# Folding the first layer's butterfly stages into its feed-forward matrices, during the attention

## The chip, the cores and the metric

The kernel runs on 1 core of one Trainium2 chip. The metric is the device time of one execution in microseconds (us). The engines of a core work side by side and are tied together by semaphores: TensorE (PE; its weight loads are PEld), VectorE (DVE), ScalarE (ACT), GpSimd (POOL) and SyncE (SP), which issues the DMA transfers. Each engine takes its own instructions in order.

## The reference, cut to what matters

Four layers work on x, 16 sequences of 256 tokens with 128 features. Each layer is `x = x + attention(norm(x)) * silu(feedforward(norm(x)))`. The change concerns the first layer alone:

```python
xn = _layernorm(x)
s = attention(xn)                 # 16 heads of 8, with relative key and query bands of 64
g = silu(ffn(xn))
x = x + s * g

def ffn(x):                       # D_HIDDEN = 512, 9 stages
    h = x @ W_exp + b_exp                       # 128 -> 512
    h = butterfly(h, up_weights, 512)           # up_weights (9, 256, 2, 2)
    h = gelu(h + up_bias)
    h = butterfly(h, down_weights, 512)
    return h @ W_con + b_con + down_bias        # 512 -> 128

def butterfly(y, weights, dim):
    for stage in range(9):                      # linear in y
        s = 2 ** stage; nb = dim // (2 * s)
        a, b = y.reshape(nb, 2, s)[0], [1]      # elements s apart
        w = weights[stage].reshape(nb, s, 2, 2)
        y = stack(w00 * a + w01 * b, w10 * a + w11 * b)
```

Both butterflies are linear. They can be multiplied into W_exp, b_exp and W_con once; the tokens then need only two matrix products and the gelu.

## The kernel before, in words

Everything is float32 with features on the 128 partitions. `build` calls the stages of all layers one after the other; each ends with a barrier of all engines. In the first layer these are `gate_and_norm`, `l0_attention`, `l0_ffn` and `gate_and_norm` again.

`l0_attention` goes through 16 sequences with 4 periods each, 64 periods and 4 to run out. Period p = 4b + r takes four heads of sequence b in four groups g. The order on each engine is written out by hand. For each period:

- TensorE: head products into the logits' banks (`logit`, L451), then per group the key's band (`add_key_band`, L458 to L461, transposes of B) and the transposes of the previous period's probabilities (`transpose`, L482), then the product with v (`weigh`, L495), and at last a new band (`bands`, L440), which waits for VectorE's last `probs_T` copy. Beside them stand the projections qk (r = 2), v and the turned sums (r = 1), the inverted sums' spread (r = 3) and the output projection (r = 0).
- VectorE: per group `add_band` (L633, adds the query's band A and finds the maximum), and for groups 0, 2 and 3 a copy of the previous period's turned probabilities (`turn`, L641). After the groups it copies half of the new band (`keep_band`, L624). At r = 1 a reciprocal of the sums (`invert`, L618) and a copy (L608) come first, at r = 3 the product `o_norm` (L614).
- ScalarE: the exponentials (L565), the copy of group 1's turned probabilities (L573), the other half of the band (L549).
- SyncE: `write(n)` sends band n to memory (L668), `windows(b, j)` fetches it back in slanted windows, four transfers into B and four into A (L687, L696). Band n is made in period n - 6.
- GpSimd: `mask_bands` cuts the windows (L716), `mask_heads(b + 2)` prepares the heads of a later sequence (L732, L734) once all logits of sequence b exist, and stands before the next sequence's masks. The first group of a period waits for its mask.

`l0_ffn` begins when the attention is over. It loads W_exp, b_exp, W_con and the biases, turns W_con by four transposes (L777), and folds the stages: SyncE spreads the weights of one stage for each of the two butterflies over all 128 rows (L803, double buffers); VectorE multiplies and adds, 12 instructions of 128x256 per stage (`stage`, L818 to L820), each waiting for the one before; GpSimd does the same for the one row of the bias, 6 per stage. Two copies, four transposes and four bias columns follow (L832, L852, L854, L860). Then a loop of four passes, each with a block of its own and a barrier, takes two chunks of 512 tokens: 4 products up (L882), 4 gelus (L902), 4 products down (L888), the last sum (L909).

Of the kernel before, what the change touches and what calls it, by code (L numbers as in the profile page):

```python
# [10 lines left out]
ALU = mybir.AluOpType  # L11
# [227 lines left out]
def l0_attention(nc, c, d, x, x_home, xn, s_out, scratch):  # L239
# [8 lines left out]
    with Scope(nc, "a0") as s:  # L248
# [9 lines left out]
        with Scope(nc, "a0t") as t:  # L258
# [100 lines left out]
         y_kept, q_masked, zeroed, masked, key_cut, logits, probs, pt_dve, pt_act, o_kept, inv_ok, *ins_) = s.sems(  # L359
            "qk_mm v_mm st_mm bc_mm y_mm band_mm logit_mm tr_mm pv_mm qk_kept v_kept lo_kept hi_kept st_sb o_ready "  # L360
            "y_kept q_masked zeroed masked key_cut logits probs pt_dve pt_act o_kept inv_ok key_in0 key_in1 key_in2 key_in3 "
            "query_in0 query_in1 query_in2 query_in3 row_out0 row_out1 row_out2 row_out3")
        key_in, query_in, row_out = ins_[:NG], ins_[NG:2 * NG], ins_[2 * NG:]
        tile = (slice(0, P), slice(P, NK))
# [27 lines left out]
        with nc.Block() as block:  # L392
# [209 lines left out]
            def _(dve):  # L602
# [39 lines left out]

                for n in range(6):
                    keep_band(n)
                for p in range(LAST + 1):
# [4 lines left out]
                    for g in range(4):  # L650
                        if p < NQ:
                            add_band(p, g)
                        if 1 <= p <= NQ and g != 1:
                            turn(p - 1, g)
                    if band_of(p) is not None:
                        keep_band(band_of(p))

            @block.sync
            def _(sp):
# [37 lines left out]

                for n in range(4):
                    write(n)
                for b in range(NSEQ):  # L700
                    for j in range(3):
                        windows(b, j)
                    if b + 1 < NSEQ:
                        write(4 * b + 4)
                        write(4 * b + 5)
                    windows(b, 3)
                    if b + 1 < NSEQ:
                        write(4 * b + 6)
                        write(4 * b + 7)
# [38 lines left out]
def l0_ffn(nc, c, d, xn, g_out):  # L748

    F, ST = 512, 9
    NF = F // P
    with Scope(nc, "f0") as s:
        up = s.sb("up", [P, F])
        dn = s.sb("dn", [P, F])
        upb = s.sb("up_bias", [1, F])
        one = s.sb("one", [1, 1])  # L760
        wc = s.sb("W_con", [P, NF, P])
        down = s.sb("down", [P, NF, P])
        bias_up = s.sb("bias_up", [P, NF])
        bias_out = s.sb("bias_out", [P, 2])
        bo = s.sb("bo", [P, 1])
        load(nc, s, [(up[:], d["W_exp"]), (upb[:], d["b_exp"].rearrange("(a n) -> a n", a=1)),
                     (wc[:], d["W_con"].rearrange("(c p) n -> p c n", p=P)), (bias_up[:], column(d["up_bias"])),
                     (bias_out[:, 0:1], column(d["b_con"])), (bias_out[:, 1:2], column(d["down_bias"]))])

        with Scope(nc, "f0t") as t:  # L770
            ps = t.banks("ps")
            turned, kept = t.sems("turned kept")
            with nc.Block() as block:
                @block.tensor
                def _(pe):
                    for i in range(NF):
                        nc.tensor.transpose(ps[:, 0, i * P:(i + 1) * P], wc[:, i, :], c["ident"][:]).then_inc(turned, 1)  # L777

                @block.vector
                def _(dve):  # L780
                    nc.vector.memset(one[:], 1.0)
                    nc.vector.tensor_tensor(bo[:], bias_out[:, 0:1], bias_out[:, 1:2], ALU.add)
                    dve.wait_ge(turned, NF)
                    nc.vector.tensor_copy(dn[:], ps[:, 0, :]).then_inc(kept, 1)
            t.barrier()

        with Scope(nc, "f0b") as t:
            wt = t.sb("stage_w", [P, 2, 2, 2 * F])
            tmp = t.sb("tmp", [P, 2, F])
            alt = t.sb("alt", [P, 2, F])  # L790
            btmp = t.sb("btmp", [1, F])
# [2550 lines left out]
```

## Time and profile before

| | us |
|---|---|
| median of 3 runs | 4407.21 (4401.78 to 4411.33) |
| the profiled execution's own time | 4403.99 |
| its span | 4402.1 |
| attention of the first layer, last result | 556.45 |
| first instruction of the next norm | 733.90 |

Busy shares of the span: PE 81%, PEld 58%, DVE 60%, ACT 48%, POOL 39%; the granted clock of TensorE is 0.907 of full speed on average. Times in the rows count from the start of the span. The span is that of the profiled execution; its own time is 1.9 us more. A timeline row has start, duration, engine, line, operation, output<-inputs, and in brackets how long the engine stood idle before and whose result ended it. A windows row has the stretch, its length, then busy time and instructions of PE, PEld, DVE, ACT and POOL, the granted clock (1.00 is 2.4 GHz, 0.50 is 1.2 GHz), the DMA engines' mean busy share and GB/s.

### The profile page before, as it was taken

The page shows a single profiled execution, that of the slowest core. Times are in us where ns is not written, and L with a number is a line of the kernel's source. Part 1 is how long each engine was busy: PE and PEld are TensorE (multiplying, and loading weights), DVE is VectorE, ACT ScalarE, POOL GpSimd, SP SyncE. Part 2 cuts the span into 40 slices and gives each one's busy share as a digit, 9 for nine tenths or more (in the row PEclk, how much of TensorE's full clock was granted, in tenths as well). Part 3 has the DMA queues.
Part 4 walks back from the last instruction along what each step waited for, and adds up shares of the span by engine and source line. Part 5 has one row for each costly group of instructions (what it writes and reads, how often), then busy time and mean ns, then how long its engine had stood idle before and what let it go on. Part 6 is the DMA issues. An engine that isn't in the chain of part 4 may idle for free. (4 is left out here: it accounts for less than half of the span.)

```text
span 4402.1 us, 79023 instructions
## 1 busy us (share of the span) xinstructions
PE 3562.2 (81%) x26972; PEld 2564.8 (58%) x26972; DVE 2629.4 (60%) x6366; ACT 2108.2 (48%) x5657; POOL 1698.5 (39%) x1896
## 2 busy tenths in 40 slices
PE   5888807656999978999996888884999999995581
PEld 2555603433666645666664888772777777774461
DVE  3666672433666645666664666663788888885233
ACT  4666604333665643544444444444666666661120
POOL 3554540303666643333330000000666666672505
PEclk7999958877999998999998999997999999996795
DMA  3777620012000000000001000001222222223122
GB/s 110 205 197 184 174 91 0 9 33 45 1 1 1 2 6 6 2 1 2 1 2 39 0 0 0 0 0 35 66 76 76 76 76 73 76 78 107 57 69 63
DMA packets 232672, 224.58 MB, mean 51 GB/s; under 512 B 59209, under 2 KB 176905, under 8 KB 232074
## 3 DMA queue, kind: packets, MB, share of 16 engines
q1 hardware_dynamic: 225642, 206.52, 16.9%
q0 software_dynamic: 4096, 8.40, 0.6%
q10 hardware_dynamic: 2592, 5.26, 0.3%
q8 instruction: 195, 3.19, 0.3%
q14 instruction: 147, 1.20, 0.1%
HBM read 166.10 MB, written 54.00 MB: 50 GB/s over the span
## 5 line engine op out<-in xcount | busy, mean ns | idle before, releaser
L2159 DVE TENSOR_TENSOR_SCAN a_h<-a_dA,a_dBu_psum 128x512 f32<-128x512 f32 x512 | 595.9, 1205 | 164.5 <-issue 105.0
L1160 POOL TENSOR_SCALAR a_probs<-a_probs,a_row_inv 128x128 f32<-128x128 f32 (+1 forms) x512 | 381.3, 762 | 324.0 <-DVE a_row_inv L1146 324.0
L2116 POOL TENSOR_TENSOR a_h<-a_h,main_g 128x512 f32<-128x512 f32 x256 | 385.1, 1506 | 270.4 <-DVE a_h L2159 260.3
L1658 DVE SCALAR_TENSOR_TENSOR m_acc<-m_o_psum,m_gate,m_acc 128x128 f32<-128x128 f32 x992 | 297.8, 346 | 116.9 <-PE m_o_psum L1622 116.5
L1883 PE MATMUL a_dBu_psum<-a_B_diag,a_dt_u_turned 64*128 64x128 f32 x4096 | 317.0, 289 | 21.6 <-DVE a_h L2159 20.8
L1622 PEld LDWEIGHTS m_o_psum<-m_values,m_hidden 128*128 128x128 f32 x2048 | 313.9, 197 | 30.0 <-ACT m_hidden L1640 2.6
L1614 PE MATMUL m_h_psum<-m_x,m_keys 128*128 128x256 f32 x1024 | 327.8, 411 | 0.0
L1640 ACT ACTIVATE m_hidden<-m_h_psum 128x256 f32<-128x256 f32 x512 | 196.2, 383 | 265.0 <-PE m_h_psum L1614 265.0
L1622 PE MATMUL m_o_psum<-m_values,m_hidden 128*128 128x128 f32 x2048 | 314.5, 280 | 0.0
L1485 POOL TENSOR_TENSOR r_position_q<-r_turned_q 128x512 f32<-128x512 f32 x128 | 159.9, 1271 | 388.9 <-DVE r_turned_q L1530 388.9
L1442 ACT ACTIVATE r_probs<-r_logits_psum,r_neg_max 128x256 f32<-128x256 f32 x512 | 235.1, 475 | 140.4 <-DVE r_neg_max L1536 140.4
L1883 PEld LDWEIGHTS a_dBu_psum<-a_B_diag,a_dt_u_turned 64*128 64x128 f32 x4096 | 257.8, 188 | 76.0 <-issue 71.2
L1904 PE MATMUL a_y_psum<-main_ident,a_h 128*128 128x128 f32 x2048 | 275.3, 276 | 7.7 <-POOL a_h L2116 6.7
L1536 DVE TENSOR_REDUCE r_neg_max<-r_logits_psum 128x2 f32<-128x512 f32 x256 | 165.0, 686 | 180.8 <-PE r_logits_psum L1352 180.8
L1904 PEld LDWEIGHTS a_y_psum<-main_ident,a_h 128*128 128x128 f32 x2048 | 230.2, 141 | 68.3 <-issue 45.8
L565 ACT ACTIVATE a_probs<-a_logits,a_neg_max 128x128 f32<-128x128 f32 (+1 forms) x512 | 225.6, 443 | 89.7 <-DVE a_neg_max L633 89.7
L1352 PE MATMUL r_logits_psum<-r_key_trig,r_position_q 64*128 64x256 f32 x2048 | 255.5, 389 | 0.0
L1753 POOL MEMSET a_flip<- 128x128 f32 x1 | 0.2, 204 | 656.1 <-POOLq L52 656.1
L1104 ACT ACTIVATE a_probs<-a_logits,a_neg_max 128x128 f32<-128x128 f32 (+1 forms) x512 | 225.2, 444 | 3.0 <-DVE a_neg_max L1126 2.2
L2023 ACT ACTIVATE a_dA<-a_dt,a_b_A 128x510 f32<-128x510 f32 x256 | 165.7, 712 | 102.1 <-DVE a_h L2159 101.4
L2023 ACT ACTIVATE a_dA<-a_dt,a_f_A 128x510 f32<-128x510 f32 x256 | 165.6, 711 | 95.2 <-DVE a_h L2159 94.4
L1352 PEld LDWEIGHTS r_logits_psum<-r_key_trig,r_position_q 64*128 64x128 f32 x2048 | 187.4, 186 | 38.6 <-issue 21.5
(540 smaller groups left out, 8244.4 us busy)
## 6 DMA issues: line engine op xcount, KB each, us to landing
main_g<-a_b_c_rows SPq DMA_DIRECT2D x256, 256.0 KB, 3.1
a_band_rows<-main_g SPq DMA_DIRECT2D x64, 512.0 KB, 3.4
a_B<-a_band_rows SPq DMA_DIRECT2D x192, 128.0 KB, 3.2
a_A<-a_band_rows SPq DMA_DIRECT2D x192, 128.0 KB, 3.1
f_x_rows<-f_zero ACTq DMA_DIRECT2D x16, 320.0 KB, 9.3
f_x_expert<-f_x_rows SPq DMA_DIRECT2D x16, 320.0 KB, 2.8
f_y_rows<-f_y_expert SPq DMA_DIRECT2D x16, 320.0 KB, 2.2
f0b_stage_w<-L_ffn_up_weights SPq DMA_DIRECT2D x9, 512.0 KB, 4.3
```

The source lines that it names most:

```text
L565: nc.scalar.activation(pr[:, k % 2, g, tile[t]], lg[:, k % 2, g, tile[t]], ACT.Exp, scale=-1.0, bias=nmax[:, k % 2, g, t:t + 1], accum_out ...
L1160: ins = nc.gpsimd.tensor_scalar(pr[:, h % NPR, tile[t]], pr[:, h % NPR, tile[t]], rinv[:, p % NST, q:q + 1], None, ALU.mult)
L1352: ins = mm(lb[:, 2 * i + a, t * T:(t + 1) * T], g_[r, k % NGB, i, half, t * P:(t + 1) * P], key_trig[r, half, :], start=False, stop=t == 1 ...
L1442: nc.scalar.activation(pr[:, k % 2, g, t, :], lb[:, g, t * T:(t + 1) * T], ACT.Exp, bias=nmax[:, k % 2, g, t:t + 1], accum_out=sums[:, b % ...
L1614: nc.tensor.matmul(hp[:, e % 3, 0:T], keys[:, e, :], tile_x[:], start=True, stop=True).then_inc(h_mm, 1)
L1622: ins = nc.tensor.matmul(op[:, f % 3, t * P:(t + 1) * P], hs[:, f % NH, t * P:(t + 1) * P], vals[:, f, :], start=True, stop=True)
L1658: ins = nc.vector.scalar_tensor_tensor(out=acc[:, t, :], in0=o, scalar=gate[:, t, e:e + 1], in1=acc[:, t, :], op0=ALU.mult, op1=ALU.add)
L1883: ins = mm(dst[:, :, tc * P + HALF * half:tc * P + HALF * (half + 1)], dtuT[U % 2][rows, q, tc, k * P:(k + 1) * P], diag[rows, M % NDIAG, ...
L1904: ins = mm(yT[:, q, tc * DI + k * P:tc * DI + (k + 1) * P], h[:, (NK * g + k) % NH, n, tc * P:(tc + 1) * P], c["ident"][:], start=False, s ...
L2023: ins = ac(dA[:, M % NDA, :, k, n, 1:], by_seq(dt[U % 2][:, k, :])[:, :, 1:], ACT.Exp, scale=W[U % 2]["A"][:, k, 2 * m + n:2 * m + n + 1])
L2116: tt(h[:, r, :, :], h[:, r, :, :], Cs[:, g % NCS, :, :], ALU.mult).then_inc(hc_pool, 1)
L2159: nc.vector.tensor_tensor_scan(flat, dA[:, M % NDA, q, k, :, :].rearrange("p n t -> p (n t)"), db[:, 2 * (g % 2) + k, :], 0.0, ALU.mult, A ...
```

## The change

A class `Butterfly` holds the tables, in buffers that exist beside the attention's. Its `ops` are 162 instructions: for each of the 9 stages 12 that alternate between `up` and the one row of `up_bias` (six each), then six for `down`. Per six the kinds are multiply, multiply, add, twice. `weights(h)` is the transfer of half-stage h (18 of them), of 512 KB, into one of two buffers. In the attention VectorE takes one op after group 0, one after group 2 and one after the band copy, in periods 0 to 53. Each op waits for the one before by a counter; the first also waits for the six loads, and the first of a half-stage for its weights. SyncE issues loads and the first two weights after `windows(0, 0..2)`, and the other 16 behind a band's write, after a wait for the counter. The bias row's work moves from GpSimd to VectorE. W_con is handed over transposed, so the first transposes go. `l0_ffn` keeps only the turning of `down`, the bias columns and the products; its eight chunks stand in one block, without loop.

```diff
+class Butterfly:
+        self.ops = []
+        for h in range(2 * self.ST):
+            i, k = h // 2, h % 2
+            for n in range(6):
+                for what in ("down",) if k else ("up", "up_bias"):
+                    self.ops.append((h, what, self.ST - 1 - i if k else i, i, n))
+    def first_of(self, h):
+        return sum(1 for op in self.ops if op[0] < h)
+    def loads(self):
+        d = self.d
+        return [(self.up[:, 0, :], d["W_exp"]), (self.down[:, 0, :], d["W_conT"]),
+                (self.up_bias[:, 0, :], d["b_exp"].rearrange("(a n) -> a n", a=1)), (self.bias_up[:], column(d["up_bias"])),
+                (self.bias_out[:, 0:1], column(d["b_con"])), (self.bias_out[:, 1:2], column(d["down_bias"]))]
+    def weights(self, h):
+        i, k = h // 2, h % 2
+        src = self.d["down_weights"][self.ST - 1 - i] if k else self.d["up_weights"][i]
+        return self.w[:, h % 2, :], src.rearrange("k r c -> (k r c)").unsqueeze(0).broadcast_to([P, 2 * self.F])
+    def turn(self, eng, op):
...
+        if n % 3 == 0:
+            return eng.tensor_tensor(m[:, :, r, :], weight(1), y[:, :, 1, :], ALU.mult)
+        if n % 3 == 1:
+            return eng.tensor_tensor(o[:, :, r, :], weight(0), y[:, :, 0, :], ALU.mult)
+        return eng.tensor_tensor(o[:, :, r, :], o[:, :, r, :], m[:, :, r, :], ALU.add)
 # l0_attention, VectorE
+                def turn_table():
+                    n, op = next(ops, (None, None))
+                    if op is None:
+                        return
+                    h = op[0]
+                    if n == 0:
+                        dve.wait_ge(table_in, 16 * len(tables.loads()))
+                    if n == tables.first_of(h):
+                        dve.wait_ge(weight_in[h % 2], 16 * (h // 2 + 1))
+                    if n:
+                        dve.wait_ge(turned_op, n)
+                    tables.turn(nc.vector, op).then_inc(turned_op, 1)
...
                         if 1 <= p <= NQ and g != 1:
                             turn(p - 1, g)
+                        if g % 2 == 0 and p < NQ:
+                            turn_table()
                     if band_of(p) is not None:
                         keep_band(band_of(p))
+                    if p < NQ:
+                        turn_table()
 # l0_attention, SyncE
+                def put_weights(h):
+                    if h >= 2:
+                        sp.wait_ge(turned_op, tables.first_of(h - 1))
+                    dst, src = tables.weights(h)
+                    sp.dma_start(dst, src).then_inc(weight_in[h % 2], 16)
+                def write_and_load(n):
+                    write(n)
+                    while due[0] is not None and (tables.first_of(due[0] - 1) - 1) // 3 <= n - 6:
+                        put_weights(due[0])
+                        due[0] = next(halves, None)
                 for b in range(NSEQ):
                     for j in range(3):
                         windows(b, j)
+                    if b == 0:
+                        for dst, src in tables.loads():
+                            sp.dma_start(dst, src, allow_slow_non_contiguous=True).then_inc(table_in, 16)
+                        put_weights(0)
+                        put_weights(1)
                     if b + 1 < NSEQ:
-                        write(4 * b + 4)
-                        write(4 * b + 5)
+                        write_and_load(4 * b + 4)
+                        write_and_load(4 * b + 5)
                     windows(b, 3)
...
 # l0_ffn, what is left
+                pe.wait_ge(made, 1)
+                for f in range(NF):
+                    nc.tensor.matmul(tp[:, 1, f:f + 1], upb[:, f * P:(f + 1) * P], one[:], start=True,
+                                     stop=True).then_inc(biased, 1)
+                for f in range(NF):
+                    nc.tensor.transpose(tp[:, 0, f * P:(f + 1) * P], dn[:, f * P:(f + 1) * P], c["ident"][:]).then_inc(turned, 1)
+                raise_(0)
+                pe.wait_ge(kept, 2)
+                for k in range(NCH):
+                    if k + 1 < NCH:
+                        raise_(k + 1)
+                    lower(k)
```

## Rows read from the trace of the kernel before

**Rows 1.** Window of the attention: us, busy us (instructions) by engine, clock, DMA share, GB/s.

```profile
83.00:556.00 473.00, 408.74 (x4008) 280.56 (x4005) 294.51 (x1320) 316.75 (x1221) 241.95 (x448) 0.97 0.72 189
```

**Rows 2.** Timeline of VectorE, 271 to 364 us: start, duration, [idle before, releaser].

```profile
271.65 0.69 DVE L624 COPY main_g<-a_transposed_psum 128x512 f32<-128x512 f32 x1 [1.31 <-PE a_transposed_psum L440]
...
278.93 0.69 DVE L624 COPY main_g<-a_transposed_psum 128x512 f32<-128x512 f32 x1 [1.31 <-PE a_transposed_psum L440]
...
285.71 0.69 DVE L624 COPY main_g<-a_transposed_psum 128x512 f32<-128x512 f32 x1 [1.31 <-PE a_transposed_psum L440]
289.44 0.29 DVE L633 CUSTOM_DVE_ANT_0 a_logits<-a_logits_psum,a_A 128x128 f32<-128x128 f32 x1 [3.04 <-POOL a_A L716]
...
294.46 0.69 DVE L624 COPY main_g<-a_transposed_psum 128x512 f32<-128x512 f32 x1 [1.31 <-PE a_transposed_psum L440]
295.07 0.34 DVE L618 RECIPROCAL a_sums<-a_sums 128x32 f32<-128x32 f32 x1
...
301.33 0.69 DVE L624 COPY main_g<-a_transposed_psum 128x512 f32<-128x512 f32 x1 [1.31 <-PE a_transposed_psum L440]
...
355.71 0.69 DVE L624 COPY main_g<-a_transposed_psum 128x512 f32<-128x512 f32 x1 [2.26 <-PE a_transposed_psum L440]
...
363.71 0.69 DVE L624 COPY main_g<-a_transposed_psum 128x512 f32<-128x512 f32 x1 [1.31 <-PE a_transposed_psum L440]
```

**Rows 3.** Timeline of TensorE, 284 to 291 us and 353 us.

```profile
284.55 1.13 PE L440 MATMUL a_transposed_psum<-a_rq_blocks,a_k 64*128 64x512 f32 x4 [0.64 <-DVE a_probs_T L641]
...
290.70 0.52 PE L482 MATMUL a_transposed_psum<-main_ident,a_probs 128*128 128x128 f32 x3 [1.80 <-DVE a_probs_T L641]
...
353.60 2.08 PE L440 MATMUL a_transposed_psum<-a_rk_blocks,a_q 64*128 64x512 f32 x4 [0.28 <-DVE a_probs_T L641]
```

**Rows 4.** Timeline of GpSimd, 282 to 289 us.

```profile
282.98 0.92 POOL L732 TENSOR_SCALAR a_k_shifted<-a_k,a_shift_k 128x256 f32<-128x256 f32 x1 [10.31 <-PE a_logits_psum L461]
...
286.95 2.37 POOL L716 TENSOR_SCALAR_AFFINE_SELECT a_A<-a_A 128x256 f32<-128x256 f32 x4
```

**Rows 5.** Timeline of the stage boundary, 555 to 558 us.

```profile
555.98 0.47 ACT L543 ACTIVATE main_s<-a_project_psum,a_vectors 128x256 f32<-128x256 f32 x1 [1.49 <-PE a_project_psum L421]
557.32 0.34 SPq L106 DMA_DIRECT2D f_up<-L_ffn_W_exp  x1
```

**Rows 6.** Timeline of VectorE in the butterfly stages, 584 to 587 us.

```profile
584.31 1.05 DVE L818 TENSOR_TENSOR f0b_tmp<-f0b_stage_w,f0b_alt 128x256 f32<-128x256 f32 x1
585.39 0.61 DVE L819 TENSOR_TENSOR f_up<-f0b_stage_w,f0b_alt 128x256 f32<-128x256 f32 x1
586.03 0.43 DVE L820 TENSOR_TENSOR f_up<-f_up,f0b_tmp 128x256 f32<-128x256 f32 x1
```

**Rows 7.** Timeline from the folded matrices to the next norm.

```profile
663.69 0.69 DVE L860 COPY f_down<-f0c_ps_psum 128x512 f32<-128x512 f32 x1 [4.72 <-PE f0c_ps_psum L854]
...
683.97 7.13 PE L882 MATMUL f_hidden_ps_psum<-main_xn,f_up 128*128 x16 [2.29 <-PEq L52]
...
698.13 0.75 DVE L909 TENSOR_SCALAR main_g<-f_y_psum,f_bo 128x512 f32 x1 [2.68 <-PE f_y_psum L888]
...
733.90 1.28 ACT L141 ACT_TABLE_LOAD   x1 [7.88 <-PEq L52]
```

**Rows 8.** Timeline of VectorE and of SyncE's DMA issues, start of the attention.

```profile
82.68 0.29 DVE L633 CUSTOM_DVE_ANT_0 a_logits<-a_logits_psum,a_A 128x128 f32<-128x128 f32 x1 [1.73 <-PE a_logits_psum L461]
...
86.06 2.55 SPq L696 DMA_DIRECT2D a_A<-a_band_rows  x4
```

**Rows 9.** Waits of SyncE's queue, 100 to 530 us (total, times, longest).

```profile
SPq L667 <- DVE main_g L624: 62.3, 14, 7.0
```

**Rows 10.** The stage weights' transfers before, from issue to landing.

```profile
DMA to landing us min/median/max: 4.2/5.4/7.4
```

**Rows 11.** Two windows of 20 us.

```profile
340.00:360.00 20.00, 17.29 (x145) 11.45 (x141) 11.43 (x51) 10.70 (x42) 14.24 (x27) 0.83 0.81 218
2460.00:2480.00 20.00, 15.73 (x87) 14.12 (x86) 11.64 (x44) 8.31 (x18) 0.00 (x0) 0.83 0.00 0
```

More of the change, by code:

```diff
@@ L241, in l0_attention @@
+def l0_attention(nc, c, d, tables, xn, s_out, scratch):
     WIN, HD, NG = 64, 8, 4
@@ L641, in turn @@
                     nc.vector.tensor_copy(pt[:, k % 2, g, :], tb[:, g % 2, 0:NK]).then_inc(pt_dve, 1)
+                ops = iter(enumerate(tables.ops))
+                def turn_table():
[10 more added lines that the diff above has]
+                    tables.turn(nc.vector, op).then_inc(turned_op, 1)
                 for n in range(6):
@@ L696, in windows @@
                         sp.dma_start(dst, src).then_inc(query_in[j], 16)
+                def put_weights(h):
[3 more added lines that the diff above has]
+                    sp.dma_start(dst, src).then_inc(weight_in[h % 2], 16)
+                halves = iter(range(2, 2 * tables.ST))
+                due = [next(halves)]
+                def write_and_load(n):
[3 more added lines that the diff above has]
+                        due[0] = next(halves, None)
                 for n in range(4):
@@ L745, in l0_attention, with l0_ffn @@
         s.barrier()
[L748 to L754 removed]
+def l0_ffn(nc, c, tables, xn, g_out):
+    F = tables.F
     NF = F // P
[L756 to L759, printed above, removed]
+    up, dn, upb = tables.up[:, 1, :], tables.down[:, 1, :], tables.up_bias[:, 1, :]
+    with Scope(nc, "f0m") as s:
         one = s.sb("one", [1, 1])
[L761 to L791, printed above, removed]
[L792 to L862 removed]
@@ L864, in l0_ffn @@
+        down = s.sb("down_T", [P, NF, P])
+        bias_up, bo = tables.bias_up, s.sb("bo", [P, 1])
         W = BANK
+        NCH = xn.shape[1] // W
         hid = s.sb("hidden", [P, 2, NF, W])
@@ L914, in l2_attention @@
+        s.barrier()
 def l2_attention(nc, c, d, xn, s_out):
@@ L3310, in build @@
         gate_and_norm(nc, c, x, xn)
-        l0_attention(nc, c, part("L0_attn"), x, d["x"], xn, s, g)
-        l0_ffn(nc, c, part("L0_ffn"), xn, g)
+        with Scope(nc, "f0") as f:
+            tables = Butterfly(f, part("L0_ffn"))
+            l0_attention(nc, c, part("L0_attn"), tables, xn, s, g)
+            l0_ffn(nc, c, tables, xn, g)
         gate_and_norm(nc, c, x, xn, s, g, gate=True)
```

180 lines of the change are left out of this document (71 added, 109 removed).

## The prediction

> **What bounds the kernel now.** I read the stage boundaries in the timeline first: the attention ends at 556.45, the next norm begins at 733.90 [rows 5, 7], and barriers part both from the rest, so the change acts up to 734 us and nothing behind it moves. What can be won is read between these two times. What must be paid is read in the attention, where the added work goes: its window shows all engines half to four fifths busy [rows 1], which tells nothing yet, since what counts is what sets its pace.
>
> VectorE's timeline answers this. Its copy of a band (L624) comes once a period, and its starts are 7.28, 6.78, 8.75 and 6.87 us apart, 29.7 us for a sequence of four periods [rows 2]; it repeats so for all 16. Three of the four periods have one loop: VectorE takes the four head groups in one piece of 3.7 us (289.44 to 294.46 less the 1.31 waited); its last copy of probs_T releases TensorE's bands, which had waited 0.64 us for it [rows 3]; bands, logits and the key's first band lead back to VectorE. So VectorE's piece lies on the path, though it is busy only 62% of the attention [rows 1]. The step of 8.75 is set by GpSimd (call the position of a period in its sequence r; this is the way from r = 3 to r = 0): its heads and masks run from 282.98 to 289.32 [rows 4], and VectorE waits 3.04 us for them [rows 2]. There TensorE waits 1.80 us [rows 3].
>
> **What it removes, after the attention.** From the attention's last result (555.98 + 0.47 = 556.45, rows 5) to the next norm's first instruction (733.90, rows 7) are 177.4 us. Of this the loads, the first transposes, the 18 half-stages, two copies and their barriers go. What stays:
> - start of a block, 0.9 us from 556.45 to 557.32 [rows 5], taken as 1.1;
> - four bias columns and four transposes: VectorE waited 4.72 for them, block start of 0.9 included, so 3.8 [rows 7];
> - eight chunks without barriers between them. A pair takes 683.97 to 698.13 = 14.16 [rows 7], of which 0.44 is the way to VectorE; four times 13.72 is 54.9. The present loop pays barrier and table load on each pair;
> - a slow clock at the start, 2.2, estimated from bands at 2.08 against 1.13 [rows 3] over four us of work; I take it in full, as the end of the attention leaves TensorE waiting;
> - the way to the last copy, the copy and the way to the norm: 0.44 + 0.75 + 0.8 = 2.0.
>
> Sum 64.0, so 113.5 are removed. If the clock stays up at the start, the 2.2 and half of the 3.8 go too, 117.
>
> **What it adds inside the attention: 162 VectorE instructions**, 108 on 128 rows and 54 on one row (same 256 columns, so the same time), three a period over periods 0 to 53. Alone, a multiplication takes 0.61 and an addition 0.43 [rows 6]. Neighbours of other tiles overlap by 0.08 (294.46 + 0.69 against 295.07, rows 2), so they add 0.53 and 0.35. The order of the list gives only multiplications to the first slot (after group 0), four of six to the second (after group 2), two of six to the third (after the band copy). The first two slots are inside the piece on the path: 0.53 + 0.47 = 1.0 a period. The third falls into VectorE's wait for the next key band (a period of 7.28 less 3.7, 1.31 and 0.69 leaves 1.6; one of 6.78 leaves 1.1, 0.4 of it taken by o_norm) or for GpSimd; only where the reciprocal of the sums follows at once (295.07), once in four periods, does it cost 0.42 [rows 2].
>
> Beside GpSimd the same multiplication took 1.05 instead of 0.61 [rows 6]: where both engines work, one waits for the other's instruction. In the attention GpSimd is busy half of the time [rows 1] and in runs, from r = 3 through r = 0 and part of r = 1. A VectorE instruction meets one under way in about five slots of twelve; the wait is the rest of a GpSimd instruction, which takes 0.6 (four in 2.37, rows 4), so some 0.28. Two of these collisions are in the chain of 282.98 to 289.32 and make it longer by 0.5 each. (The Trainium skill, SBUF — State Buffer, Who interferes with whom, says that a VectorE instruction with two SBUF inputs and a GpSimd one that reads SBUF exclude each other for the whole instruction. By this rule the collisions count; were they free, the sum per sequence would be 3.4 instead of 5.3. The trace agrees: 1.05 against 0.61.)
>
> Per sequence: r = 0: 1.0 + 0.55; r = 1: 0.42 + 1.0 + 0.28; r = 2: 1.0; the GpSimd period: 1.0 (VectorE's own way there has 1.8 us to spare, as TensorE's wait of 1.80 shows, which covers its slots). Sum 5.25, over 53 periods = 13.25 sequences: 70 us. Bounds: 45 without any collision (3.42 a sequence); 130 if every instruction costs what it cost beside a busy GpSimd, 1.0 (2.0 in each of three periods, 0.9 before the reciprocal, 2.9 in GpSimd's chain).
>
> **What it moves: the loads.** SyncE issues windows of sequence 0 until 88.6 [rows 8]; the six loads and the first weights stand behind them. VectorE's first added instruction stands behind group 0 of period 0, at about 83.4 (82.68 and two reductions, rows 8), and waits for both. Six loads take some 2.7 us to issue (0.34 the first, rows 5, those of columns more), and weights landed 5.4 us after issue, 4.2 to 7.4 [rows 10]. So the first weights are there at 88.6 + 2.9 + 5.4 = 96.9, and VectorE stands for 13 us with groups 1 to 3 behind it, and ScalarE and TensorE behind those. GpSimd gets ahead meanwhile, so its hold on the early periods (up to the 3.04 of rows 2) goes into it, and the half clock after so long a pause adds something: 12 net, 9 to 17.
>
> The other 16 weight transfers (0.5 MB each, 8.4 MB where the attention moves 189 GB/s times 473 us = 89 MB, rows 1) I cost at nothing. SyncE waits 62.3 / 14 = 4.4 us a sequence for bands now [rows 9]; each transfer is issued about two periods (14 us) before its first use and lands in 4 to 7. SyncE's new wait, for VectorE's counter, is for an instruction one further than the band that it has just written, so about 1 us; windows stand behind it, GpSimd's masks wait for those, but GpSimd's critical chain starts from the logits and not from a window (282.98 waited for logits_psum, rows 4). If that cover went, each of 16 would cost some 5 us.
>
> **The clock.** TensorE's clock fell to half in four of the fourteen periods with the 1.80 us wait; the bands then took 2.08 instead of 1.13 [rows 3], and the next period 8.00 instead of 6.87 (355.71 to 363.71, rows 2): 2.1 us together. After the change TensorE waits 1.6 to 2.0 us in every period. All the attention is at 0.97 now [rows 1]; the stretch of this fall is at 0.83, so 0.17 x 2 x 20 = 6.8 us at half clock cost 2.1, 0.3 each; a later stage where TensorE is busy 79% is at 0.83 too [rows 11]. TensorE's busy share goes from 86% to some 75%: nothing to 36 us more (0.86 of clock over some 550 us instead of 0.97, so 120 us more at half). I take 12, since only four waits of this length in fourteen brought the clock down, and some of the cost falls where GpSimd sets the pace.
>
> **Sum.** -113.5 + 70 + 12 + 12 = -19.5. The profiled execution took 4403.99 (span 4402.1, 1.9 around it), so 4384.5; the median of before is 3.2 above its profiled execution, so 4387.7; I predict 4387.
>
> **Rivals.**
> - *The collisions cost little* (GpSimd's instructions let VectorE's through, or fall elsewhere): -113.5 + 45 + 12 + 8 = -48, 4359. For it: most of GpSimd's work of a sequence lies in one run. Against it: rows 6. Chance 0.16.
> - *The clock falls in most periods*: -113.5 + 70 + 14 + 36 = +6, 4413, no change. For it: the clock of 0.83 where TensorE is busy for a like share [rows 11]. Against it: ten of fourteen waits of 1.80 us left it alone. Chance 0.17.
> - *The other side: VectorE and GpSimd serialise.* If each added instruction meets a GpSimd one, as it did in the table stages, the attention pays 130 and the result is -113.5 + 130 + 12 + 12 = +40, 4447. It decides from 7 us a sequence on, against my 5.25. Against it: GpSimd is idle in half of the slots. With partly met ones (from 4416): chance 0.14.
> - *The change hides everything* (the slots fill VectorE's idle 38%): about 4300. Against it: TensorE's waits for the last copy in each period [rows 3]. Chance 0.03.
>
> **How the numbers follow.** My forecast has 0.50, its own range 4370 to 4404, the others 0.16, 0.17, 0.14 and 0.03. The clock and collision rivals together bring the range for 8 in 10 to 4352 to 4425. This kernel's measurement tells 0.2%, 8.8 us, from no change: 4398.4 to 4416. Faster: 0.43 of my forecast, 0.05 of the clock's, 0.16 and 0.03, together 0.67; same: 0.07 of mine, 0.11 of the clock's, 0.18; slower: 0.01 + 0.14, 0.15.
>
> **What the profile will show.** The stretch from the attention's last result to the next norm at 62 to 66 us, TensorE without a gap of more than 1 us in it. A wait of VectorE of 12 to 14 us near 83 us for the weights' transfer. Steps of the band copy of about 8.6, 8.3, 8.0 and 10.0 instead of 6.9, 7.3, 6.8 and 8.75 while the tables are made, and the old ones in the last ten periods. Added multiplications at 0.61 where GpSimd rests and up to 1.2 where it works. I am wrong if the steps grow by under 0.8 or over 2 a period, if the clock of the attention is below 0.9, or if VectorE waits for weights after the first ones.

## The result, and the profile after

The changed kernel takes 4358.22 us (median of four runs, 4349.31 to 4360.85) against 4404.49 for the kernel before beside it (4396.62 to 4411.33): ratio 0.9892, 95% interval 0.9869 to 0.9915. It is faster by about 46 us, or 1.1%, where I forecast 20, and lies below my own range of 4370 to 4404, inside the one for 8 in 10 (4352 to 4425). Its profiled execution took 4349.31, so the two profiled executions are 54.7 apart; that difference is what is taken apart below.

The attention's window and the stretch behind it, changed kernel (columns as in rows 1):

```profile
83.00:556.00 473.00, 349.54 (x3373) 241.34 (x3372) 332.08 (x1273) 280.75 (x1034) 231.21 (x394) 0.96 0.73 189
624.00:685.00 61.00, 58.26 (x140) 26.45 (x140) 7.03 (x12) 23.12 (x35) 0.00 (x0) 0.97 0.00 0
```

In the same 473 us TensorE and ScalarE did less than in [rows 1] (349.54 us against 408.74), VectorE more: the attention is stretched. The clock is 0.96 against 0.97, and the mean DMA rate is the same 189 GB/s.

VectorE's timeline, first the start, then one sequence of four periods; L684 is the band copy, L291 to L294 are the added instructions:

```profile
82.27 0.42 DVE L693 CUSTOM_DVE_ANT_0 a_logits<-a_logits_psum,a_A 128x256 f32<-128x256 f32 x1
82.61 0.08 DVE L693 DVE_READ_ACCUMULATOR2_ANT a_neg_max<- 128x1 f32 x1
96.53 0.61 DVE L291 TENSOR_TENSOR f_tmp<-f_stage_w,f_up 128x256 f32<-128x256 f32 x1 [13.83 <-DMA f_stage_w<-L_ffn_up_weights]
...
209.48 0.69 DVE L684 COPY main_g<-a_transposed_psum 128x512 f32<-128x512 f32 x1 [1.31 <-PE a_transposed_psum L500]
...
212.77 0.62 DVE L291 TENSOR_TENSOR f_tmp<-f_stage_w,f_up 128x256 f32<-128x256 f32 x1
...
214.88 0.59 DVE L291 TENSOR_TENSOR f_bias_tmp<-f_stage_w,f_up_bias 1x256 f32<-1x256 f32 x1
...
217.80 0.69 DVE L684 COPY main_g<-a_transposed_psum 128x512 f32<-128x512 f32 x1 [1.31 <-PE a_transposed_psum L500]
218.41 0.60 DVE L293 TENSOR_TENSOR f_up<-f_stage_w,f_up 128x256 f32<-128x256 f32 x1
...
225.43 0.69 DVE L684 COPY main_g<-a_transposed_psum 128x512 f32<-128x512 f32 x1 [1.31 <-PE a_transposed_psum L500]
...
228.71 0.29 DVE L693 CUSTOM_DVE_ANT_0 a_logits<-a_logits_psum,a_A 128x128 f32<-128x128 f32 x1 [1.99 <-PE a_logits_psum L521]
...
231.85 0.71 DVE L293 TENSOR_TENSOR f_down<-f_stage_w,f_down 128x256 f32<-128x256 f32 x1
...
234.89 0.69 DVE L684 COPY main_g<-a_transposed_psum 128x512 f32<-128x512 f32 x1 [1.31 <-PE a_transposed_psum L500]
...
243.29 0.69 DVE L684 COPY main_g<-a_transposed_psum 128x512 f32<-128x512 f32 x1 [1.31 <-PE a_transposed_psum L500]
```

The stall at the start is there, 13.83 us, for the weights. Then the band copies are 8.32, 7.63, 9.46 and 8.40 us apart, where [rows 2] has 7.28, 6.78, 8.75 and 6.87. Two of the three added instructions of a period stand ahead of the last copy of probs_T, the third behind the band copy. Behind period 53, without table instructions, the last four steps are the old ones (577.64 to 584.50 is 6.86). Of the signs that I named for being wrong, VectorE waits for no weights after the first ones, the clock is over 0.9, and the steps grow by 1.03 in the mean, though the one behind 225.43 by 0.71, under my 0.8.

TensorE's timeline, same kernel:

```profile
224.26 1.13 PE L500 MATMUL a_transposed_psum<-a_rq_blocks,a_k 64*128 64x512 f32 x4 [1.48 <-DVE a_probs_T L701]
229.97 0.52 PE L542 MATMUL a_transposed_psum<-main_ident,a_probs 128*128 128x128 f32 x3 [1.45 <-DVE a_probs_T L701]
233.73 1.13 PE L500 MATMUL a_transposed_psum<-a_rk_blocks,a_q 64*128 64x512 f32 x4 [1.78 <-DVE a_probs_T L701]
```

Its wait for VectorE's last copy was 0.64 [rows 3] and is now 1.48 in the same place: the two slots ahead of that copy add to the path.

GpSimd's timeline, same kernel, and its groups over 100 to 570 us (the last columns are busy us, mean ns):

```profile
221.84 0.92 POOL L833 TENSOR_SCALAR a_k_shifted<-a_k,a_shift_k 128x256 f32<-128x256 f32 x1 [11.82 <-PE a_logits_psum L521]
222.74 2.39 POOL L835 TENSOR_SCALAR a_q_masked<-a_q,a_mask,a_shift_q_masked 128x256 f32<-128x256 f32 x4
225.09 0.99 POOL L817 TENSOR_SCALAR_AFFINE_SELECT a_B<-a_B 128x512 f32<-128x512 f32 x2
226.05 2.54 POOL L817 TENSOR_SCALAR_AFFINE_SELECT a_A<-a_A 128x256 f32<-128x256 f32 x4
```

```profile
L817 POOL TENSOR_SCALAR_AFFINE_SELECT a_A<-a_A 128x512 f32<-128x512 f32 x159 | 107.2, 690 | 7.6
L835 POOL TENSOR_SCALAR a_q_masked<-a_q,a_mask,a_shift_q_masked 128x256 f32<-128x256 f32 x56 | 33.6, 612 | 0.0
```

The chain from the first head to the end of the fourth mask of A takes 226.05 + 2.54 - 221.84 = 6.75 us, against 6.34 in [rows 4]. Between these two ends the kernel before has:

```profile
283.88 2.16 POOL L734 TENSOR_SCALAR a_q_masked<-a_q,a_mask,a_shift_q_masked 128x256 f32<-128x256 f32 x4
285.99 1.00 POOL L716 TENSOR_SCALAR_AFFINE_SELECT a_B<-a_B 128x512 f32<-128x512 f32 x2
```

So the masked heads are longer by 0.23 us and the masks of A by 0.17 (2.54 against 2.37), the rest is as before. A mask of A takes 690 ns in the mean; with the same filter over 100 to 550 us of the kernel before it was 634, a masked head 555. Of the 162 table instructions 85 run while one of GpSimd's does.

VectorE's own instructions hardly suffer (counts, then min/median/max ns):

```profile
L291 DVE TENSOR_TENSOR f_tmp<-f_stage_w,f_up x18: 606/620/640, 96.5 to 524.1; 128x256 f32<-128x256 f32 x18
L291 DVE TENSOR_TENSOR f_tmp<-f_stage_w,f_down x18: 615/626/1001, 128.4 to 549.6; 128x256 f32<-128x256 f32 x18
```

The end of the attention and the feed-forward, by ScalarE, VectorE and TensorE:

```profile
623.53 0.47 ACT L603 ACTIVATE main_s<-a_project_psum,a_vectors 128x256 f32<-128x256 f32 x1 [1.49 <-PE a_project_psum L481]
...
684.84 1.28 ACT L141 ACT_TABLE_LOAD   x1 [7.65 <-PEq L52]
```

```profile
625.08 1.05 PE L885 MATMUL f0m_turned_psum<-f0m_one,f_up_bias 1*128 1x1 f32 x8 [1.58 <-DVE f0m_one L909]
626.05 1.01 PE L888 MATMUL f0m_turned_psum<-main_ident,f_down 128*128 128x128 f32 x4
626.85 8.41 PE L872 MATMUL f0m_hidden_ps_psum<-main_xn,f_up 128*128 128x512 f32 x16
```

```profile
645.60 0.75 DVE L918 TENSOR_SCALAR main_g<-f0m_y_psum,f0m_bo 128x512 f32<-128x512 f32 x1 [6.04 <-PE f0m_y_psum L880]
652.47 0.75 DVE L918 TENSOR_SCALAR main_g<-f0m_y_psum,f0m_bo 128x512 f32<-128x512 f32 x1 [6.12 <-PE f0m_y_psum L880]
```

The attention ends at 624.00, 67.6 later than before [rows 5]; the next norm begins at 684.84. The stretch between is 60.84, under my 62 to 66, against 177.45 [rows 5, 7]. TensorE's one gap of over 1 us in it is the first, 1.58. A chunk takes 6.87 us.

**The balance** between the two profiled executions, with attention steps summed from the starts of the band copies. "Regular" is 13 sequences at the median of each of the four steps; what the same 52 steps took beyond it is "irregular".

```
                                         forecast   measured
stretch after the attention               -113.5     -116.6
regular steps (per sequence 5.25 / 4.13)   +70        +53.7
start                                      +12        +15.2
irregular steps (forecast: the clock)      +12         +0.1   (6.8 after, 6.7 before)
first copy and tail of the attention         0         -1.3
all behind the next norm                     0         -5.6
sum                                        -19.5      -54.5   (-54.7 unrounded)
```

### The profile page after: what moved, and what is told of

Read it like the earlier page. It is cut to its first block and busy times, and to the rows that moved or that the text cites. A ratio compares the mean times of both kernels' runs of the same rounds, so it can differ in the third digit from the quotient of the medians.

```text
span 4347.6 us, 78783 instructions
## 1 busy us (share of the span) xinstructions
PE 3550.6 (82%) x26968; PEld 2561.0 (59%) x26968; DVE 2628.9 (60%) x6417; ACT 2116.3 (49%) x5654; POOL 1665.8 (38%) x1841
```

## The experiments

The kernels below were timed in three groups, each beside runs of the kernel before, and ratios are to those. Those took 4431.0 us for the first four kernels below, 4404.27 for the next four and 4434.39 for the last two, so times of different groups, and the times in us that I expected, are compared by ratio or stage. "Steps" are the medians to r = 2, 3, 0, 1; in the kernel before they are 7.28, 6.78, 8.75, 6.86, in the changed one 8.33, 7.63, 9.46, 8.39.

**Loads ahead of the pipeline.** The six loads and first two weight transfers are issued before SyncE's loop and not inside it.

```diff
+                for dst, src in tables.loads():
+                    sp.dma_start(dst, src, ...).then_inc(table_in, 16)
+                put_weights(0)
+                put_weights(1)
...
-                    if b == 0:
-                        for dst, src in tables.loads(): ...
-                        put_weights(0)
-                        put_weights(1)
```

> Only the six loads and the first two weight transfers move: SyncE issues them before the first band's write instead of after the first twelve window transfers. My theory (VectorE's wait of 13.8 us near 83 us is for these transfers alone, and 15 us of the attention's 67.5 us are its price): the wait is gone, the attention ends 12 to 15 us earlier, time about 4344. Rival (the windows and GpSimd's masks set the pace of the first periods anyway, VectorE waited 3.4 us for them in period 1 before the change): the gain is 11 us or less. Second rival (the early transfers delay the first bands' way): the first group of period 0 starts later than 82.05.

Measured: 4369.24 us, ratio 0.9857 (0.9842 to 0.9872). The stall is gone: the two steps from 80 us on take 14.8 us together where the changed kernel needs 28.9 and the kernel before 13.8. But the attention ends at 615.47, only 8.5 earlier: under the 12 to 15 of the theory and in the range of the rival, though not by its cause, since the two steps gave 14.1 back. The ratio's interval overlaps that of the changed kernel. Regular steps are unchanged (33.86 us a sequence); irregular ones take 11.3 us beyond them, where the changed kernel had 6.8. Two of them, 9.64 and 10.34, follow each other from 171 us on, where the clock is at 0.66 (170 to 180 us).

**Slots moved into waits.** Of the three table instructions of a period, two are issued between the last copy of probs_T and the band copy, and one behind that.

```diff
-                        if g % 2 == 0 and p < NQ:
-                            turn_table()
+                    if p < NQ:
+                        turn_table()
+                        turn_table()
                     if band_of(p) is not None:
                         keep_band(band_of(p))
```

> The same 162 instructions, other places: two after VectorE's last copy of a period and before the band copy, where it waits 1.31 us for TensorE, one after the band copy as before. My theory (the cost is the two slots inside the piece that TensorE waits for): the steps of the band copy go back to about 6.9 + 0.4, 7.3, 6.8 and 8.75 to 9.1, the attention is some 45 us shorter, time about 4313, and the wait at the start costs a few us less, since it stands behind period 0's groups. Rival (VectorE's work itself or its meeting with GpSimd costs, wherever it stands): the steps stay at 9.5, 8.4, 8.3 and 7.7, time about 4358.

Measured: 4332.49, ratio 0.9780 (0.9765 to 0.9795); steps 7.28, 6.78, 9.43, 7.38, the attention ends at 573.98. The same 162 instructions cost nothing at two of the four steps. What is left is 0.7 us at the GpSimd step, over the 0 to 0.35 that I expected and what the rival had there, and 0.5 at the step with the reciprocal. Of the 50.0 us by which the attention ends earlier, 38.4 are these steps, 5.0 the start (the wait for weights is 11.23 instead of 13.83) and 6.2 irregular steps, of which 0.3 us are left.

**Both together.**

> Both edits of the two runs before. If their costs are independent: the attention ends 10 to 15 us before that of the slots alone, time 4295 to 4303. If GpSimd or the windows become the limit, the steps of the first sequence stay long and the time is above 4308.

Measured: 4324.90, ratio 0.9761 (0.9748 to 0.9775), attention's end 565.20, 8.8 before that of the moved slots alone where I expected 10 to 15; steps 7.28, 6.78, 9.42, 7.38. VectorE's timeline of it, around a band copy:

```profile
301.22 0.61 DVE L291 TENSOR_TENSOR f_tmp<-f_stage_w,f_down 128x256 f32<-128x256 f32 x1
301.87 0.61 DVE L293 TENSOR_TENSOR f_down<-f_stage_w,f_down 128x256 f32<-128x256 f32 x1
302.62 0.69 DVE L684 COPY main_g<-a_transposed_psum 128x512 f32<-128x512 f32 x1
303.22 0.42 DVE L294 TENSOR_TENSOR f_down<-f_down,f_tmp 128x256 f32<-128x256 f32 x1
303.56 0.35 DVE L678 RECIPROCAL a_sums<-a_sums 128x32 f32<-128x32 f32 x1
```

Where 1.31 us were waited for TensorE's band [rows 2] stand two multiplications. On VectorE only the addition ahead of the reciprocal (303.22) delays something. The GpSimd step is longer by what GpSimd's chain is longer: 0.67 and 0.66 (7.00 us against 6.34). The two groups that are slower in it:

```profile
229.59 2.65 POOL L835 TENSOR_SCALAR a_q_masked<-a_q,a_mask,a_shift_q_masked 128x256 f32<-128x256 f32 x4
232.20 1.17 POOL L817 TENSOR_SCALAR_AFFINE_SELECT a_B<-a_B 128x512 f32<-128x512 f32 x2
```

**Two weight transfers only.** The other 16 are not issued; the table instructions go on with the weights of the first two transfers.

```diff
-                    if n == tables.first_of(h):
+                    if n == tables.first_of(h) and h < 2:
...
-                halves = iter(range(2, 2 * tables.ST))
+                halves = iter(range(0))
```

> The changed kernel without the 16 later weight transfers: all half-stages multiply with the first two weights (left out: the other weights, so the tables are others). My theory (these transfers are hidden): every step of the band copy as in the changed kernel within 0.1 us, time 4350 to 4362. Rival (the transfers slow the windows, GpSimd's masks wait longer, and SyncE's wait for VectorE's counter holds back windows): the attention ends 5 us or more earlier.

Measured, one run: 4377.50, attention's end 621.58 against 624.00, steps 8.33, 7.64, 9.47, 8.43. The steps are those of the changed kernel; 2.4 us is within what its irregular steps vary by.

**No table instructions, all transfers.** SyncE waits for the transfer before in the same buffer instead of for VectorE's counter.

```diff
-                            turn_table()
...
-    up, dn, upb = tables.up[:, 1, :], tables.down[:, 1, :], tables.up_bias[:, 1, :]
+    up, dn, upb = tables.up[:, 0, :], tables.down[:, 0, :], tables.up_bias[:, 0, :]
```

> The changed kernel with all transfers of the tables and weights kept, but none of VectorE's 162 table instructions; the first layer's feed-forward takes the unmultiplied matrices, so its result leaves the butterfly out. Theory (the attention's added time outside the start is those instructions, the transfers are hidden): the band copies' steady steps return to 7.28, 6.78, 8.75 and 6.87 us, the attention ends at 558 to 566 us (before: 556.5; with the instructions and two weight transfers: 621.6). Rival (the transfers cost time of their own beside the attention): steps stay over those by 0.2 us or more each, and the end lies at 575 or later. The next layer norm follows 60 to 61 us after the attention's end in both.

Measured, one run: 4287.85; steps 7.28, 6.79, 8.75, 6.86; attention's end 554.58, just below the 558 to 566 expected, the next norm at 615.4. The 16 later weight transfers beside the attention cost nothing that shows. The loads at the start do: one step, from 100.02 to 111.75, is 11.73 us long where the kernel before has 6.37. GpSimd and VectorE in it:

```profile
102.45 1.00 POOL L816 TENSOR_SCALAR_AFFINE_SELECT a_B<-a_B 128x512 f32<-128x512 f32 x2 [9.20 <-DMA a_B<-a_band_rows]
106.73 0.29 DVE L693 CUSTOM_DVE_ANT_0 a_logits<-a_logits_psum,a_A 128x128 f32<-128x128 f32 x1 [6.02 <-PE a_logits_psum L521]
```

SyncE issues the six loads and two weights from 87.99 to 92.15 us, the windows stand behind them, and GpSimd waits for the windows: these masks begin at 102.45, against 95.75 in the kernel before and 95.84 with the loads ahead of the pipeline. In the changed kernel VectorE's stall of 13.83 us covers this.

**The product's one block alone**, in the kernel before.

```diff
-        PER = 2
-        with nc.Fori(0, xn.shape[1] // (W * PER) or 1) as i:
-            per = min(PER, xn.shape[1] // W)
-            with nc.Block() as block:
+        NCH = xn.shape[1] // W
+        with nc.Block() as block:
...
-                    for k in range(per):
+                for k in range(NCH):
```

> The kernel before with one part of the change alone: the feed-forward's two products with their eight chunks in one block, in place of a block of their own each time; the butterfly stages stay passes over the activations after the attention. Theory (my sum gave some 10 us of the stretch after the attention to this part): the stretch from the attention's end to the next table load falls from 177.4 to 166 to 168 us, and the ratio to the kernel before is 0.9974 to 0.9980. Rival (all of the 116.6 us comes from the nine passes up and nine down that go away): 176 to 178 us, ratio 0.9995 to 1.0005.

Measured: the stretch is 717.9 - 549.9 = 168.0 as the theory had it, 9.4 less. But the whole takes 4405.08, ratio 1.0001 (0.9992 to 1.0010), and in its profile the later stages take the gain back in small pieces (first to third table load 2243.8 us instead of 2235.6). The stretch is the theory's, the ratio the rival's (0.9995 to 1.0005); neither foresaw both.

**Table instructions with one input.**

```diff
-            return eng.tensor_tensor(m[:, :, r, :], weight(1), y[:, :, 1, :], ALU.mult)
+            return eng.tensor_scalar(m[:, :, r, :], weight(1), 0.5, None, ALU.mult)
(and so the other two)
```

> The changed kernel with each of the 162 table instructions turned into a product of the same strided stage weight with a constant, written to the same place: one input from SBUF in place of two, same count, places in the order, waits and shape of result; the matrices are left out of the table, so the result is not the butterfly's. Theory (the part of the step to r = 0 that is over 8.75 us, +0.71, is GpSimd made slower while VectorE reads two inputs from SBUF, its chain 6.75 against 6.34 us): GpSimd's short masks are back at 1.00 us, the chain at 6.3 to 6.45, the step to r = 0 at 8.75 to 8.9, and the other three stay over their old values by the instructions' own durations (if these stay at 0.6 us: 8.3, 7.6, 8.3; if one input takes half the time: about 7.9, 7.2, 7.6). Rival (GpSimd is late for another reason, its later start behind VectorE or the DMA traffic): the chain stays at 6.7 to 6.8 and the step to r = 0 at 9.3 to 9.5.

Measured: 4345.25, ratio 0.9862 (0.9847 to 0.9877); steps 7.87, 7.38, 9.52, 8.05. Undisturbed the instruction takes 0.39 instead of 0.62, and three steps shrink by 0.46, 0.25 and 0.34. The GpSimd step does not. GpSimd's timeline of it:

```profile
221.07 1.25 POOL L833 TENSOR_SCALAR a_k_shifted<-a_k,a_shift_k 128x256 f32<-128x256 f32 x1 [10.00 <-PE a_logits_psum L521]
222.31 2.17 POOL L835 TENSOR_SCALAR a_q_masked<-a_q,a_mask,a_shift_q_masked 128x256 f32<-128x256 f32 x4
224.43 1.00 POOL L817 TENSOR_SCALAR_AFFINE_SELECT a_B<-a_B 128x512 f32<-128x512 f32 x2
225.38 2.53 POOL L817 TENSOR_SCALAR_AFFINE_SELECT a_A<-a_A 128x256 f32<-128x256 f32 x4
```

The chain is 6.84 long here, and so in nine of thirteen sequences; in four it is 6.54. The rival's numbers came out within 0.04, though not for its reason: the slowed instruction is now the first (1.25 instead of 0.92), a one-input instruction holds GpSimd up as well, and without any table instruction the step is 8.75. Over the whole attention it holds it up less: a mask of A takes 660 ns in the mean, against 690 with two inputs and 634 before.

**The third slot away from the reciprocal**, on top of the version with both: none behind the band copy of r = 0, two behind that of r = 3.

```diff
                     if p < NQ:
-                        turn_table()
+                        for _ in range((0, 1, 1, 2)[p % NG]):
+                            turn_table()
```

> The version with the loads ahead and two table instructions ahead of each band copy, and of the third ones, the one that stands ahead of the reciprocal of the sums is moved to behind the r = 3 copies, where VectorE waits 3.3 us for a mask. Theory (the step to r = 1 is still long by 0.5 us because the reciprocal and all behind it start one instruction late): that step goes from 7.38 to 6.9, the others stay at 7.26, 6.78 and 9.5, the attention ends at 558 to 560 us in place of 565.2, the ratio to the kernel before is 0.9745 to 0.975. Rival (the moved instruction hits GpSimd's masks there and lengthens its chain by what the other step gains): the step to r = 0 at 9.8 to 10.0, the attention's end within 2 us of 565.

Measured: 4296.22, ratio 0.9752 (0.9739 to 0.9766); steps 7.28, 6.78, 9.73, 6.86; attention's end 563.65. Its GpSimd timeline:

```profile
226.81 0.92 POOL L834 TENSOR_SCALAR a_k_shifted<-a_k,a_shift_k 128x256 f32<-128x256 f32 x1 [6.17 <-PE a_logits_psum L521]
227.72 2.73 POOL L836 TENSOR_SCALAR a_q_masked<-a_q,a_mask,a_shift_q_masked 128x256 f32<-128x256 f32 x4
230.40 1.36 POOL L818 TENSOR_SCALAR_AFFINE_SELECT a_B<-a_B 128x512 f32<-128x512 f32 x2
231.72 2.36 POOL L818 TENSOR_SCALAR_AFFINE_SELECT a_A<-a_A 128x256 f32<-128x256 f32 x4
```

The step to r = 1 is at its old length, as the theory said, but the instruction set down in VectorE's wait meets the masked heads (2.73 where the version with both has 2.65) and the short masks (1.36 for 1.17). The chain is 7.27 long instead of 7.00 and the GpSimd step 0.3 longer: most of the gain goes back, and the attention ends 1.6 earlier, within the rival's 2. The interval overlaps that of the version with both; each of the two beats both kernels.

**The products in four blocks again**, in the changed kernel, and **the changed kernel unedited** beside it. The diff is that of the one block alone, reversed, with the bias columns and transposes in a block ahead.

> The changed kernel with the feed-forward's products in the form of the kernel before (four blocks of two chunks each, the bias and transposes in a block ahead of them); the attention and the tables as changed. The kernel before with one block of eight chunks had its stretch shortened by 9.3 us, but its whole time was the same (ratio 1.0001, interval 0.9992 to 1.0010). Theory (the one block is worth some 9 us of the stretch, and something behind it gives them back): the stretch from the attention's end to the next table load is 70 to 72 us in place of 60.8, and the ratio to the kernel before lies within 0.001 of that of the changed kernel on the same chip. Rival (the 9 us reach the end here, and the missing gain of the other run was a chance of its later stages): the same stretch, and a ratio 0.002 over that of the changed kernel.

> The changed kernel without any edit, on the same chip as the version with four blocks, as what that is compared with: ratio 0.987 to 0.991, attention's end at 618 to 626 us, stretch 60.8 us, the time from the table load behind it to the next two 2230 to 2245 and from there to the end 1426 to 1438 us (so far these two varied in that way between kernels whose later stages are the same).

Measured: 4391.80, ratio 0.9907 (0.9892 to 0.9921), stretch 693.45 - 620.18 = 73.3; unedited 4382.97, ratio 0.9884 (0.9868 to 0.9901), stretch 691.06 - 630.23 = 60.8. The medians are 8.8 us apart, as the rival has it, but the intervals overlap. In the unedited kernel the attention ended at 630.23, outside what I expected, with 11.6 us of irregular steps, and the stages from the third table load on took 1454.6 us against the 1426 to 1438 expected. The kernel before is slower in this group too. In all profiles of this group and the first these last stages take 1452 to 1459 us, in the others, the two of the first comparison and the second group, 1429 to 1437. Where the irregular steps lie, the windows of the unedited kernel show (the last columns are the clock, DMA share, GB/s):

```profile
284.00:340.00 56.00, 41.34 (x413) 28.50 (x413) 40.01 (x154) 33.04 (x121) 30.36 (x52) 1.00 0.83 206
340.00:400.00 60.00, 48.87 (x396) 35.13 (x395) 40.73 (x154) 34.40 (x129) 20.42 (x35) 0.83 0.63 162
400.00:440.00 40.00, 30.35 (x304) 20.43 (x303) 27.93 (x104) 23.34 (x85) 22.63 (x39) 1.00 0.68 171
```

From 337 to 385 us, most of it in the window with a clock of 0.83, five steps took 9.19, 9.78, 9.58, 10.47 and 8.98 instead of 8.4, 8.32, 7.64, 9.49 and 8.4. TensorE is busy 48.87 of 60 us there; that it is the bound in such a stretch fits, but no run took it apart. In all these profiles, every step over 0.5 us longer than usual either has a granted clock below 1.00 or follows right behind one that has; the step of 11.73 us above has its own cause.

## Why the forecast was right in sign and short in size

**What bounds the attention** was read rightly. VectorE's piece sets three steps: its instructions cost their length inside the piece and nothing in its waits (slots moved: 7.28 and 6.78 again; no instructions: all four old steps). GpSimd sets the fourth.

**The stretch** was -113.5 and is -116.6. The chunks and the way out were priced right: from the first up-product 58.0 us (626.85 to 684.84) against 54.9 + 2.2 + 2.0 = 59.1. The bias and the transposes with the block's start took 2.85 (624.00 to 626.85) against 4.9; I had taken the old wait of 4.72 [rows 7], in which transposes and products alternated with the clock at half.

**The step that failed is the price of collisions in the per-sequence sum**, 5.25 against 4.13: of the 35 us between forecast and measured balance, 16 lie here and 12 in the clock. The steps to r = 2, 3, 0, 1 grew by 1.05, 0.85, 0.71 and 1.52; I had named steps of 8.3, 8.0, 10.0 and 8.6, which grow by 5.15 and do not match my sum one by one. The sum has 1.0 for r = 2 and 1.7 for the step with the reciprocal, both near what came; its other 2.55, for r = 0 and the GpSimd chain, stand against the 1.56 of the steps to r = 3 and 0. I lengthened the chain by 1.0 (two collisions of 0.5). Both collisions came, at 0.23 and 0.17, and it grew by 0.41 (6.75 against 6.34). The rest of that step's growth is VectorE's piece: behind the masks it takes 6.18 us (228.71 to 234.89) instead of 5.02 (289.44 to 294.46, rows 2), while the chain starts 3.59 instead of 2.73 ahead of the band copy. I had also let VectorE wait 0.28 in five of twelve slots; 85 of 162 instructions do meet one of GpSimd's, so the share was right, but VectorE's multiplications kept a median of 0.62. The price is paid mostly by GpSimd (690 ns a mask against 634), which has time to spare except in its chain. The table stages of the kernel before were the wrong row to price this from: there two engines, both without any pause, did the same two-input work. The Trainium skill (SBUF — State Buffer, Who interferes with whom) says that the losing engine is locked out for the whole instruction; here what a meeting with a two-input instruction adds to a group of GpSimd's is 0.17 and 0.23 us in the chain of the changed kernel, less than the 0.6 of the instruction met. A meeting can begin late in either instruction, so this does not refute the rule; it shows that my half microsecond was too much, and no run came near my 130 us bound.

**The start**, 12, was 15.2 (the wait itself 13.83, forecast 13). I had netted some of it against GpSimd's lead; the runs do not show such a gain. That it is the loads' place in the queue is shown by the first experiment, which took the wait away. That this bought 8.5 us and not 14 is mostly from irregular steps (4.5 us more of them), whose sum varied from run to run. What the forecast left out is that the loads also push back the windows behind them, which cost 5.4 us in the run without table instructions and is hidden under the wait here.

**The clock**, 12, was nothing in this execution: irregular steps 6.8 us against 6.7 before. The waits of TensorE that I forecast came, 1.0 to 2.0 us in every period, but they did not lower its clock much more often (0.96 against 0.97). A long fall does cost: the five steps of the unedited kernel's second profile are 5.8 us over their usual length. Over the profiles with the slots of the changed kernel (unedited twice, early loads, two transfers, four blocks) irregular steps are 3.1, 4.0, 6.8, 11.3 and 11.6 us. At the old pace they are 6.7 in the kernel before, 1.5 in its version with one block, and 1.9 without table instructions, the step of 11.73 left out. The means are 7.4 and 3.4, so the term is nearer 4 than 12, and single executions put it at -4 to +10; that it came to nothing in the two executions compared is chance. In the two versions with moved slots, where TensorE waits 0.64 us again in most periods, irregular steps are 0.3 and 0.0. What tips the clock is not settled: in the changed kernel a wait of 1.96 us at 438.92 stood ahead of a window at 0.89 (440 to 460 us), one of 1.78 at 233.73 ahead of one at 1.00 (240 to 260 us).

**Nothing behind the norm moves**: the profiled executions differ by 5.6 us there, 1.4 of it from first to third table load and 4.0 behind. In all the kernels here, which share that code, the first part took 2232.7 to 2243.8 us, and the second 1428.6 to 1437.2 in those timed beside a kernel before of 4404; the difference is within this scatter. The medians are 46.3 apart and the profiled executions 54.7: that of the changed kernel, 4349.31, was the fastest of its four.

**What stays open** is the worth of the product's one block. Its stretch is 9 to 12 us shorter in both pairs; in the kernel before nothing of this reached the end, in the changed kernel 8.8 us did, with overlapping intervals. A cause was not found, and scatter of the later stages explains the profile of the first pair but not the median of its ten runs. What tips the clock, and so the irregular steps, is open too.

Of the rivals, "the collisions cost little" came nearest (4359), though by a middle sum of collisions (4.13, between 3.42 and 5.25) and no cost of the clock. The serialising rival needed 7 us a sequence.

## What to carry to other kernels

Work that is moved under another stage costs what it adds to that stage's slowest loop, not its busy time: 162 instructions cost 53.7 us with two of three between the copies that TensorE waits for, and 15.3 (30.86 - 29.68 a sequence, 13 times) with these two where VectorE waits for TensorE. A place that looks free on its own engine can still lengthen another engine's chain. Transfers issued at the back of a busy queue are late by the queue, and make what stands behind them late; put those that are needed once at the start ahead of the loop.

## What was not expected of the hardware

Added VectorE instructions beside GpSimd cost far less in the attention than in the table stages: VectorE's multiplication has a median of 0.60 to 0.63 here and took 0.76 to 0.86 in the mean there, and GpSimd's groups grow by 0.2 to 0.6. A one-input VectorE instruction (0.39 us) delays GpSimd too: its chain is 6.84 in most sequences, against 6.75 with two inputs (0.62 us), but over the attention a mask is longer by 26 ns in the mean instead of 56. And 9.4 us taken from one stage did not show in the whole kernel's time, so a stage's gain of 0.2% has to be measured at the end as well.
